# Nine tiles of source rows fetched row by row on SyncE's queue in a graph attention kernel

## The reference, cut to what matters

```python
h = jnp.maximum(_layernorm(x), 0.0)                  # 12500 nodes x 128
q = (h @ Wq.T + bq).reshape(N, 8, 16);  v = (h @ Wv.T + bv).reshape(N, 8, 16)
k = (edge_attr @ Wk.T + bk).reshape(-1, 8, 16)       # 212500 edges, sorted by dst
qs, qd = q[src], q[dst]
in_m, out_m, diag_m = (qs * k).sum(-1), (qd * k).sum(-1), (qs * qd).sum(-1)
score = sum(segment_softmax(m / 4, dst) for m in (in_m, out_m, diag_m)) * distance ** lam
out = x + leaky_relu(segment_sum(score[..., None] * v[dst], dst) @ Wo.T + bo)
```

## Time and profile before

| | us |
|---|---|
| three runs | 2353.46, 2354.01, 2349.38; median 2353.46 |
| the profiled execution's own time | 2350.5 |
| its span, first to last instruction | 2348.7 |
| mean granted TensorE clock | 0.878 of full speed |
| edge pass, SP's first transfer to PE's last pick | 120.3 to 2172.6 |

### The profile page before, as it was taken

How to read it: one execution, slowest core, us unless ns; L and a number is a source line. 1 busy time by engine, 2 the same in 40 slices (tenths; PEclk the granted TensorE clock), 3 DMA queues, 4 the chain that set the end, 5 groups by cost and what they waited for, 6 DMA issues and landing times. The chain is left out here.

```text
span 2348.7 us, 38637 instructions
## 1 busy us (share of the span) xinstructions
PE 1789.8 (76%) x11148; PEld 1098.0 (47%) x11148; DVE 1818.6 (77%) x3163; ACT 917.7 (39%) x1931; POOL 1693.7 (72%) x1772
## 2 busy tenths in 40 slices
PE   5568888877777787778887887877777777777377
PEld 5535544444444444444554544444444444444145
DVE  7669998778878777878878777777887877888465
ACT  8124444434434334334434333444433434443121
POOL 0677777777777777777777777777777777777374
PEclk9889999989989989889889889898998999998576
DMA  6798888677767777777677777777777776773354
GB/s 232 233 289 256 271 248 268 210 222 237 229 213 232 230 232 230 228 229 232 215 218 234 220 219 228 232 231 226 230 229 229 231 229 214 235 215 115 109 164 152
DMA packets 380483, 522.46 MB, mean 222 GB/s; under 512 B 68963, under 2 KB 288625, under 8 KB 366962
## 3 DMA queue, kind: packets, MB, share of 16 engines
q1 hardware_dynamic: 288258, 228.18, 32.4%
q10 hardware_dynamic: 35664, 179.21, 21.5%
q0 software_dynamic: 56352, 112.60, 17.4%
HBM read 435.16 MB, written 84.57 MB: 221 GB/s over the span
## 5 line engine op out<-in xcount | busy, mean ns | idle before, releaser
L153 POOL DMA_INDIRECT qsrc<-q_tab,idx_sb x1661 | 1589.7, 957 | 513.6 <-issue 499.9
L829 PE MATMUL qd_ps<-onehot,window 128*128 128x128 f32 x3328 | 526.3, 309 | 138.1 <-DVE onehot L1042 132.7
L935 ACT COPY kq<-qd_ps 128x512 f32<-128x512 f32 x416 | 242.7, 583 | 852.0 <-PE qd_ps L829 831.8
L829 PEld LDWEIGHTS qd_ps<-onehot,window 128*128 128x128 f32 x3328 | 473.3, 219 | 211.7 <-issue 204.2
L1056 DVE TENSOR_TENSOR prod<-qs_ps,kq 128x1024 f32<-128x1024 f32 x416 | 506.2, 1217 | 4.1 <-PE qs_ps L838 2.6
L818 PE MATMUL k_ps<-ea_sb,wk_sb 128*128 128x512 f32 x832 | 492.1, 677 | 12.7 <-DMA ea_sb<-in_ea 12.7
L838 PE MATMUL qs_ps<-ident,qsrc 128*128 128x128 f32 x1664 | 281.4, 296 | 287.1 <-DMA qsrc<-q_tab,idx_sb 285.4
L1052 DVE SCALAR_TENSOR_TENSOR prod<-k_ps,bk_col,kq 128x512 f32<-128x512 f32 x416 | 310.2, 746 | 129.0 <-PE lg_ps L807 117.9
L838 PEld LDWEIGHTS qs_ps<-ident,qsrc 128*128 128x128 f32 x1664 | 203.7, 151 | 369.7 <-issue 359.8
L807 PE MATMUL lg_ps<-prod,heads 128*32 128x384 f32 x3328 | 366.0, 513 | 1.1 <-DVE prod L1056 1.1
L929 ACT ACTIVATE kq<-k_ps,bk_col 128x512 f32<-128x512 f32 x416 | 285.6, 687 | 206.2 <-PE k_ps L818 204.8
(11 more groups left out here) (170 smaller groups left out, 1163.1 us busy)
## 6 DMA issues: line engine op xcount, KB each, us to landing
ea_sb<-in_ea ACTq DMA_DIRECT2D x104, 1024.0 KB
window<-q_tab SPq DMA_DIRECT2D x1664, 64.0 KB
state<-rows ACTq DMA_DIRECT2D x104, 576.0 KB
near_sb<-near_tab SPq DMA_DIRECT2D x104, 512.0 KB
pa_sb<-pa_tab SPq DMA_DIRECT2D x104, 258.0 KB, 8.1
qsrc<-q_tab,idx_sb POOLq DMA_INDIRECT x1661
xs<-in_x SPq DMA_DIRECT2D x15, 448.0 KB, 4.9
q_tab<-qs SPq DMA_DIRECT2D x14, 448.0 KB, 2.5
```

Of the source, the lines that this page charges most:

```text
L153: pool.indirect_dma_start(out=qsrc[0:n, r, j, :], out_offset=None, in_=q_tab, in_offset=bass.IndirectOffsetOnAxis(ap=idx_sb[0:n, u // QUAD ...
L829: t = nc.tensor.matmul(qd_ps[:, at], window[:, r, j, :], onehot[:, m % 2, at], start=True, stop=True)
L935: nc.scalar.copy(kq[:, m % 2, 1, :], qd_ps[:, :]).then_inc(qd_copied, 1)
```

## The change

Nine tiles are no longer gathered by POOL. They are the first tile of the last group of units 14, 25, 36 and so on to 102 (`TAKEN`). For each of them SP issues 128 DMAs of one row of 512 bytes into a new SBUF tile `hand` (two buffers), three of them (`EACH`) behind the four window DMAs of each group, so over 11 units (`SPAN`) a tile. The fetching of the first starts in unit 2, and the last ends in unit 100. The row numbers come from a new input, `hand_idx`, held in one partition (`hand_i`), and three of them are read into registers ahead of each three DMAs. PE waits for all 128 rows of a taken tile and transposes `hand` in the place of `qsrc`. The other 1652 tiles are gathered as before.

```diff
+EACH = 3
+SPAN = -(-P // (EACH * NG))
+HAND = [2 + SPAN * i for i in range(9)]
+TAKEN = [u + SPAN + 1 for u in HAND]
...
+def by_hand(u, g, j):
+    return u in TAKEN and (g, j) == (NG - 1, 0)
...
 def gathered(u, g, j):
+    if by_hand(u, g, j):
+        return 0
...
+        hand = sb("hand", [P, 2, F])
+        hand_i = sb("hand_i", [1, len(HAND) * P], I32)
+        hand_in = [sem(f"hand_in{k}") for k in range(2)]
...
+            sp.dma_start(env["hand_i"][:, :], env["hand_idx"]).then_inc(bases_in, 16)
...
+            def fetch_rows(u, g):
+                i = max(k for k in range(len(HAND)) if HAND[k] <= u)
+                first = (u - HAND[i]) * EACH * NG + g * EACH
+                n = min(EACH, P - first)
+                if n <= 0:
+                    return
+                if first == 0 and i > 1:
+                    sp.wait_ge(qs_turned, NG * (TAKEN[i - 2] + 1))
+                _, row = nc.values_load_multi_w_load_instructions(
+                    hand_i[0:1, bass.ds(i * P + first, n)], engines=(mybir.EngineType.SP,),
+                    min_val=0, max_val=N - 1, skip_runtime_bounds_check_because="src is a node's number")
+                for k in range(n):
+                    sp.dma_start(hand[first + k:first + k + 1, i % 2, :], q_tab[bass.ds(row[k], 1), :]
+                                 ).then_inc(hand_in[i % 2], 16)
...
                     for j in range(GRP):
                         sp.dma_start(window[:, r, j, :], q_tab[bass.ds(base[j], P), :]).then_inc(window_in[r], 16)
+                    if HAND[0] <= u < HAND[-1] + SPAN:
+                        fetch_rows(u, g)
...
                 for j in range(GRP):
-                    t = nc.tensor.transpose(qs_ps[:, m % 2, j * P:(j + 1) * P], qsrc[:, r, j, :], ident[:, :])
+                    rows_in = qsrc[:, r, j, :]
+                    if by_hand(n // NG, n % NG, j):
+                        i = TAKEN.index(n // NG)
+                        pe.wait_ge(hand_in[i % 2], 16 * P * (i // 2 + 1))
+                        rows_in = hand[:, i % 2, :]
+                    t = nc.tensor.transpose(qs_ps[:, m % 2, j * P:(j + 1) * P], rows_in, ident[:, :])
```

More of the change, by code:

```diff
@@ L84, in need, with gnn_kernel @@
         eng.wait_ge(sem, n)
-def gnn_kernel(nc, x, idx, dst_ext, tile_first, ea, dist, wqvT, bqv, wkT, bk, woT, bo, lam,
+def gnn_kernel(nc, x, idx, hand_idx, dst_ext, tile_first, ea, dist, wqvT, bqv, wkT, bk, woT, bo, lam,
                ident_in, iota_in, ramp_in, node_in, heads_in, tri_in, bit_in, shift_in, out):
@@ L582, in edge_pass @@
         "idx_sb", "idx_first", "idx_in", "qsrc", "q_in", "fetch_sources", "fetch_results"))
-    q_tab, idx, ea, state, state_u, near_tab, pa_tab = (env[k] for k in (
-        "q_tab", "idx", "ea", "state", "state_u", "near_tab", "pa_tab"))
+    q_tab, idx, ea, state, state_u, near_tab, pa_tab, hand, hand_i, hand_in = (env[k] for k in (
+        "q_tab", "idx", "ea", "state", "state_u", "near_tab", "pa_tab", "hand", "hand_i", "hand_in"))
     with ExitStack() as ctx:
@@ L728, in _ @@
             env["nodes_done"](sp)
-            sp.wait_ge(env["bases_in"], 16)
+            sp.wait_ge(env["bases_in"], 32)
+            def fetch_rows(u, g):
[12 more added lines that the diff above has]
+                                 ).then_inc(hand_in[i % 2], 16)
             def unit(h, q):
@@ L1554 @@
     ea = by_unit(padded(g["edge_attr_128"], EPAD, 0)).transpose(3, 0, 5, 2, 1, 4)
+    listed = by_unit(src).transpose(4, 3, 0, 2, 1).reshape(P, NCOL, NG, GRP)
     arrays = {
         "x": padded(g["x"], NPAD, 0),
-        "idx": by_unit(src).transpose(4, 3, 0, 2, 1).reshape(P, NCOL * SUP),
+        "idx": listed.reshape(P, NCOL * SUP),
+        "hand_idx": listed[:, TAKEN, NG - 1, 0].T.reshape(1, len(TAKEN) * P),
         "dst_ext": np.concatenate([np.concatenate([np.full(G, -G, dst.dtype), dst])[:EPAD].reshape(P, T)[:, 0:G],
```

## The result

The changed kernel takes 2545.5 us (median of 4 runs, 2542.7 to 2553.7), the kernel before 2351.4 in the same session (4 runs): a ratio of **1.084 (95% interval 1.081 to 1.086)**, 194 us slower. The forecast was 2342 with a range up to 2380.

What follows compares the result with a forecast made beforehand. POOL's stream of gathers was taken as the bound: nine gathers less save 11.4 us, SP's 637 us of new work fits its 684 us of cover at no cost, so 2342 us from 2353.5, range 2336 to 2380.

Steps and rivals of the forecast that it cites:

- The bound before, POOL's stream: POOL's gathers, 1.262 us each, set the time from about 420 us; nine fewer save 11.4 us.
- The price of a row DMA: On SP's queue, one-row DMA with address work: 0.436 us, bounded by 0.30 and 0.516; 1152 make 502 us.
- the sum: SP's added work: 502 us of row DMAs and 135 of register loads, together 637 us against 684 of cover.
- the prediction's shorter wording: On SP's row DMAs: a transfer whose slowest dimension is 1 runs on one DMA engine; the issuer writes the other 15 increments.
- the 387 register loads: On SP's queue, loads of row numbers at 0.35 us each, 135 us in all.
- the 47 us that the sum left over: SP's room: 684 us of cover less 637 of new work, or 0.041 us a row.
- The hold-ups that I hoped to lose: Delays of SP's window DMAs; some should go because rows let the windows' queue drain; no size given.
- The break-even: On SP's queue, a row at 0.477 us: below it no cost, above it 11.5 us per 0.01 us a row.
- Case (b): SP's queue becomes the bound and TensorE's picks wait for windows: up to 2387 us, chance 0.23.
- Case (c): Transfers, not their issue, limit the gathers, so nothing is gained: 2353.5 us; chance 0.12 with the narrow case of (b).
- The first units: At the start SP's lead goes after some ten units, TensorE then runs at SP's 19.3 us a unit; no cost.
- POOL's line: The pace of POOL's gathers, 20.2 us a unit, which TensorE meets at about unit 35 in place of 18.

Runs made afterwards that it cites:

- e5: The changed kernel with one load of twelve row numbers a unit in place of three a group: 2333.7 us, ratio 0.995.
- e8: As e5, but the load of twelve ahead of a unit's groups and the row DMAs ahead of each group's window DMAs: 2333.3 us, ratio 0.9948.
- e9: As e8, but all sixteen window numbers of a unit come in one load ahead of its groups: 2335.7 us, ratio 0.9962.
- e12: The kernel before with its table of window numbers moved by one value, so loads of four start off 16 bytes; no rows: 2340.2 us.
- e11: As e5, but each row of 512 bytes is written as sixteen pieces to sixteen partitions, not one piece to one: 2367.3 us.
- e2: The changed kernel, but each load of row numbers reads four values from a multiple of four, not three from anywhere: 2394.7 us.
- e4: The changed kernel, but one load a group reads four window numbers and three row numbers together: 2677.0 us, ratio 1.144.
- e6: The changed kernel, still three row numbers a load, but each load starts at a multiple of four: 2547.7 us.
- e7: As e2, four values a load, but each load starts one value behind a multiple of four: 2620.4 us.

## Why the prediction was wrong, point by point

- **The bound before, POOL's stream: right.** Nine gathers less are worth 11 us once SP keeps up: e5, e8 and e9 lie 10.9, 11.1 and 7.6 us under the kernel before, for a forecast of 11.4. e12 shows the other side, 267 us more on SP's queue and no change.
- **The price of a row DMA: right.** Forecast 0.436 us from two rows of the trace; measured 510 / 1152 = 0.443. The statement of the Trainium skill ("DMA: Bandwidth & Descriptors", section "Why a DMA increments its semaphore by 16 and not by 1") that the issuing sequencer writes the other fifteen increments had no term in the sum. How many engines take part goes there by the slowest dimension that isn't of size 1, as the instruction carries it; the trace has a row DMA as one element of 512 bytes, so the prediction's shorter wording comes to the same here. The trace agrees with it as far as it shows: 999 semaphore updates stand there for 512 row DMAs of one buffer, two each, against 3152 for 208 window DMAs, 15 each, and 7312 for 512 of the sixteen-piece DMAs of e11. The row DMA is cheap all the same, and the load behind it pays. That the fifteen increments are the cause of this surcharge fits e11, but no run shows it.
- **The failed step: the 387 register loads.** I took 0.35 us each from the row of the window loads and gave it no upper end, while I bounded the row DMA with care. That row is one of loads of four values from a multiple of four. The new loads are of three. They measured 327 / 387 = 0.84 us on average, 327 us in place of 135. With the 47 us that the sum left over, this alone put SP 145 us over. Loads of four from a multiple of four take 162 us in e2, so 165 of the 192 us too little are the form of the load. The other 27 are that I took the row's median: the window loads of the kernel before take 169 / 396 = 0.43 us each with their steps, and 387 at that price are 165 us.
- **A cost that the sum did not have**: the loads of window numbers, old work that I took as unchanged, rose from 169 to 257 us behind the row DMAs. That is 88 us more. The hold-ups that I hoped to lose gave back 38. The 50 left are again more than the 47 us of room, so the right price for the new loads alone would not have saved the forecast: e2 has the cheap loads and takes 2394.7 us.
- **The break-even was right in form.** 2342 + (887 - 684) = 2545 us is what the prediction's own sum gives with the measured occupation; measured 2545.5. So close a match is chance: the same sum for e2, e4, e6 and e7, from the kernel before beside them, falls 4 to 18 us short. Case (b) was the right mechanism with the wrong cause: its price was written on the row DMA alone, so its worst was 2387, and the range ended at 2380. With an upper end for the load as well, the range would have been far wider, and a change that spends 93% of a queue's slack on a guess would have deserved less than 0.65.
- **Case (c)** did not occur. The gathers didn't get shorter or longer, and the same bytes by another queue did bring the gain in e5.
- **The first units: right in kind, wrong in size.** SP's lead is lost and TensorE meets POOL's line later, without harm, but not at unit 35. The sum itself gives 12.8 + 6.4 = 19.2 us a unit (the prediction has 19.3). At 19.3 (e8) they meet about unit 60, at 19.6 (e5) about 95, at 18.5 (e9) about 25. SP's lead was gone by unit 5, and not after ten units: the last window of unit 1 is issued only some 15 us ahead of its pick, where later in the pass of before it is 34 to 38.

## What to carry to other kernels

When work goes to a queue that only issues, sum every instruction of it, the register loads as well, and bound the price of each kind from both sides; a row of the trace prices a load only for the same number of values and the same start. Work that was cheap in the place before can become dearer by what is put ahead of it. And a queue at 96% of the pace has no room for a guess: take the version that needs fewer instructions (one aligned load a unit) before the one that is nearest to the code.

## What the runs showed of the hardware

- A register load on SP (TENSOR_LOAD from SBUF) took 0.302 us for four values from a multiple of four, 0.754 for twelve, 0.972 for sixteen: about 0.08 us and 0.22 for each four. It took 0.675 for three values, at a multiple of four or not, and 0.875 for four that start one value behind a multiple, so some 0.20 us for each single value (medians; some loads take up to 3 us).
- The first register load after DMAs of one piece in one partition took 0.19 to 0.26 us more (0.562 against 0.302; 0.947 against 0.754), even with four other DMAs between; not after DMAs of the same bytes in sixteen pieces (0.300).
- On SP's queue a DMA of one row of 512 bytes took 0.249 us, one of sixteen pieces 0.331, one of 128 rows 0.333.
